# Sliding-window attention with value products that leave queries on partitions, in an order of its own on every engine

## The reference, cut to what matters

```python
qkv = (x @ W_qkv + b_qkv).reshape(B, S, 3, HEADS, HD)      # B=32, S=125, HEADS=8, HD=16
# per head: scores of each query with the keys at most 32 rows away, softmax over them
p = softmax(where(near, q @ k.T * HD ** -0.5, -inf))
attn = p @ v                                               # per head (125, 16)
return attn @ W_proj + b_proj                              # added to h
```

## Time and profile before

| | us |
|---|---|
| median of 3 runs | 592.61 (591.25 to 595.72) |
| profiled execution, its own time | 590.11 |
| its span, first to last instruction or transfer | 588.3 |
| PE / PEld busy | 505.1 / 352.7 |
| DVE / ACT / POOL busy | 417.8 / 371.5 / 272.4 |

### The profile page before, as it was taken

One profiled execution on the slowest core, in us unless ns is written; L12 is line 12 of the kernel. 1 busy time (PEld: TensorE's weight loads), 2 busy tenths in 40 slices (PEclk: granted clock), 3 DMA queues, 4 the chain that ended last, 5 costly groups with the idle time before them and its releaser, 6 DMA issues.

```text
span 588.3 us, 13845 instructions
## 1 busy us (share of the span) xinstructions
PE 505.1 (86%) x4554; PEld 352.7 (60%) x4554; DVE 417.8 (71%) x1694; ACT 371.5 (63%) x1115; POOL 272.4 (46%) x218
## 2 busy tenths in 40 slices
PE   6997999999986999999989999976888888888830
PEld 4686666676654666666666666644666666666510
DVE  3798578888854688878888887635777777777750
ACT  5975588889874344454444445436788888888740
POOL 2760677878865766666665666421111111111030
PEclk9999599999996999999999999986999999999965
DMA  4441122222220000000000000000000000000013
GB/s 153 141 138 37 43 50 59 62 58 59 63 70 29 26 21 31 20 19 20 17 19 20 30 4 1 2 0 0 2 1 3 2 2 2 2 2 2 2 38 103
DMA packets 21914, 19.87 MB, mean 34 GB/s; under 512 B 14180, under 2 KB 18436, under 8 KB 21716
## 3 DMA queue, kind: packets, MB, share of 16 engines
q1 hardware_dynamic: 21268, 18.28, 11.0%
q10 hardware_dynamic: 576, 0.71, 0.4%
HBM read 16.81 MB, written 2.18 MB: 32 GB/s over the span
## 4 chain that ended last, share of the span: by engine, by line
PE 25%; ACT 19%; DVE 9%; POOL 7%; issue 6%; DVEq 0%; ACTq 0%; POOLq 0%
ACT wprobs L977 10%; PE bank L829 6%; DVE n L1112 5%; PE quad L784 4%; POOL hb L1060 3%; POOL hb L1058 3%; PE quad L852 3%; PE bank L909 3%; ACT wprobsT L1003 2%; PE quad L776 2%; ACT oF L995 2%; PE bank L858 2%; ACT woT L1010 2%; ACT ao L942 1%; PE quad L807 1%
## 5 line engine op out<-in xcount | busy, mean ns | idle before, releaser
L476 POOL TENSOR_SCALAR put<-keyb,c 100x1000 f32<-100x1000 bf16 x32 | 89.1, 2784 | 43.6 <-DMA keyb<-key_scratch 27.8
L1078 POOL TENSOR_TENSOR kbd<-wkT,c 128x250 f32<-128x250 f32 x32 | 19.3, 602 | 134.1 <-ACT wkT L985 134.1
L977 ACT ACTIVATE wprobs<-quad,wmax 125x125 f32<-125x125 f32 x256 | 73.1, 384 | 1.8 <-DVE wmax L1166 0.7
L1166 DVE CUSTOM_DVE_ANT_0 quad<-quad,c 125x125 f32<-125x125 f32 x256 | 65.7, 320 | 11.6 <-PE quad L852 8.0
L609 ACT ACTIVATE probs<-quad,negmax 100x250 f32<-100x250 f32 x128 | 58.4, 468 | 19.8 <-DVE negmax L561 18.6
L784 PE MATMUL quad<-h1T,w 128*128 128x500 f32 x128 | 60.7, 598 | 0.4 <-ACT hid L948 0.3
L807 PE MATMUL quad<-w,hid 128*125 128x128 f32 x512 | 59.0, 273 | 0.1
L807 PEld LDWEIGHTS quad<-w,hid 128*125 128x125 f32 x512 | 57.4, 188 | 0.9 <-issue 0.5
L948 ACT ACTIVATE hid<-quad,vec_cols 128x500 f32<-128x500 f32 x64 | 43.0, 676 | 9.8 <-PE quad L784 8.1
L491 PE MATMUL bank<-c,probs 100*125 100x100 f32 x256 | 46.8, 309 | 2.2 <-ACT probs L609 1.4
L491 PEld LDWEIGHTS bank<-c,probs 100*125 100x125 f32 x256 | 35.5, 202 | 19.9 <-issue 12.2
(11 more groups left out here) (138 smaller groups left out, 1227.1 us busy)
## 6 DMA issues: line engine op xcount, KB each, us to landing
keyb<-key_scratch SPq DMA_DIRECT2D x64, 97.7 KB
xa<-xT SPq DMA_DIRECT2D x8, 500.0 KB, 3.6
xt<-xtok SPq DMA_DIRECT2D x16, 250.0 KB
out<-o_all SPq DMA_DIRECT2D x4, 500.0 KB
w<-weights SPq DMA_DIRECT2D x1, 1024.0 KB, 7.3
vec_rows<-rows SPq DMA_DIRECT2D x1, 448.0 KB, 5.4
c<-consts ACTq DMA_DIRECT2D x1, 428.5 KB, 5.9
w<-weights ACTq DMA_DIRECT2D x1, 192.0 KB, 4.4
```

The costliest lines, as they stand in the source:

```text
L476: nc.gpsimd.tensor_scalar(put[u % 3][:, :, :], keyb[p][:, :, :], c[0:ROWS, CONST["sidx"]], None, ALU.is_equal).then_inc(put_done, 1)
L977: ins = nc.scalar.activation(probs[p][:, j, :], s_of(j), ACT.Exp, bias=negmax[p][:, j:j + 1], scale=-1.0)
L1166: ins = nc.vector.tensor_tensor_reduce(s_of(j), s_of(j), c[0:LH, CONST["band"]], 1.0, OFF, ALU.add, ALU.min, negmax[p][:, j:j + 1])
```

## The change

The value product of a head has the transposed probabilities (125 columns) as the stationary operand and the values (now 16 columns and a single column of ones, `VW` = 17) as the moving one. The result has queries on partitions, and the row sum in column 16 of each head. The copy `oT` on ACT and the two transposes L909 go. Reciprocal and normalisation read the products at once, one step later (at the head of DVE's step). The projection writes into the bank of keys, queries and values, with added waits of ACT and PE on `z_done`. `oF` is made by DVE, not ACT. On PE the transpose of `otok` moves behind the transposes of heads 4 to 7, and the projection to between the transposes of heads 0 to 3 and the value products. On ACT the copy of heads 4 to 7 moves between the exponentials of heads 0, 1 and those of heads 2, 3. On DVE z moves behind the minima of heads 4 to 7 and the copy of transposed probabilities ahead of the statistics. The diff, cut to its core:

```diff
 PE
                 if within(u, 2, B + 2):
-                    pe.wait_ge(otok_done, u - 1)
-                    nc.tensor.transpose(y_of, otok[:, :], ident[0:LH, 0:LH]).then_inc(oF_ready, 1)
...
                 if within(u, 2, B + 2):
-                    pe.wait_ge(oF_done, u - 1)
-                    nc.tensor.matmul(y_proj, oF[:, :], w[:, WEIGHT["wp"]], start=True, stop=True).then_inc(proj_ready, 1)
+                    pe.wait_ge(otok_done, u - 1)
+                    nc.tensor.transpose(y_of, otok[:, :], ident[0:LH, 0:LH]).then_inc(oF_ready, 1)
...
+                if within(u, 2, B + 2):
+                    pe.wait_ge(oF_done, u - 1)
+                    pe.wait_ge(v_done, min(u + 1, B))
+                    wait(pe, z_done, u - 2)
+                    nc.tensor.matmul(x_proj, oF[:, :], w[:, WEIGHT["wp"]], start=True, stop=True).then_inc(proj_ready, 1)
+
                 if within(u, 1, B + 1):
-                    wait(pe, z_done, u - 1)
+                    wait(pe, oF_done, u - 1)
                     pe.wait_ge(pT0_done, u)
                     pe.wait_ge(pT1_done, u)
                     pe.wait_ge(v_done, u)
...
                     for j in range(H):
-                        ins = nc.tensor.matmul(y_bank[CW * (j % 4):CW * (j % 4) + CW, LH * (j // 4):LH * (j // 4) + LH],
-                                               vo[pm][:, j, :], probsT[pm][:, j, :], start=True, stop=True)
+                        ins = nc.tensor.matmul(y_o[:, j, :], probsT[pm][:, j, :], vo[pm][:, j, :], start=True, stop=True)
                     ins.then_inc(pv_ready, 1)
-
-                if within(u, 1, B + 1):
-                    pe.wait_ge(oT_done, u)
-                    for i in range(2):
-                        ins = nc.tensor.transpose(y_a[:, 128 * i:128 * i + 128], oT[:, LH * i:LH * i + LH], ident)
-                    ins.then_inc(otok_ready, 1)
 ACT
+                    wait(act, z_done, u - 2)
                     nc.scalar.activation(kT[:, :], x_k, ACT.Identity, bias=col("wk_b")).then_inc(kT_done, 1)
...
-                if within(u, 2, B + 2):
-                    act.wait_ge(oF_ready, u - 1)
-                    wait(act, proj_ready, u - 2)
-                    nc.scalar.activation(oF[:, :], y_of, ACT.Identity, bias=col("wv_b")).then_inc(oF_done, 1)
                 if within(u, 0, B):
                     wait(act, pT0_ready, u - 1)
                     exponents(0)
-                    exponents(1)
                 if within(u, 1, B + 1):
                     act.wait_ge(pT1_ready, u)
                     wait(act, pv_ready, u - 2)
                     nc.scalar.activation(probsT[1 - p][:, 4:8, :]...).then_inc(pT1_done, 1)
                 if within(u, 0, B):
+                    exponents(1)
                     exponents(2)
                     exponents(3)
-                if within(u, 1, B + 1):
-                    act.wait_ge(pv_ready, u)
-                    wait(act, otok_ready, u - 1)
-                    nc.scalar.activation(oT[:, :], y_bank[:, 0:2 * LH], ACT.Copy).then_inc(oT_done, 1)
 DVE, its whole step in the new order
+                if within(u, 2, B + 2):
+                    dve.wait_ge(pv_ready, u - 1)
+                    wait(dve, otok_done, u - 2)
+                    nc.vector.reciprocal(rinv[:, :], y_o[:, :, HD]).then_inc(rinv_done, 1)
+                    dve.wait_ge(rinv_done, u - 1)
+                    wait(dve, oF_ready, u - 2)
+                    nc.vector.tensor_tensor(otok..., y_o[:, :, 0:HD], rinv..., ALU.mult).then_inc(otok_done, 1)
+                if within(u, 0, B):
+                    dve.wait_ge(scores, u + 1)
+                    mask_and_min(0, 4)
+                if within(u, 2, B + 2):
+                    dve.wait_ge(oF_ready, u - 1)
+                    wait(dve, proj_ready, u - 2)
+                    nc.vector.tensor_scalar(oF[:, :], y_of, col("wv_b"), None, ALU.add).then_inc(oF_done, 1)
+                if within(u, 0, B):
+                    mask_and_min(4, 8)
                 if within(u, 2, B + 2):
                     dve.wait_ge(proj_ready, u - 1)
-                    nc.vector.tensor_tensor(z_all..., y_proj.unsqueeze(1), z_all..., ALU.add).then_inc(z_done, 1)
+                    nc.vector.tensor_tensor(z_all..., x_proj.unsqueeze(1), z_all..., ALU.add).then_inc(z_done, 1)
+                if within(u, 0, B):
+                    dve.wait_ge(pT0_ready, u + 1)
+                    wait(dve, pv_ready, u - 1)
+                    nc.vector.tensor_copy(probsT[p][:, 0:4, :]..., t_bank[0]...).then_inc(pT0_done, 1)
                 if within(u, 2, B + 2):
                     dve.wait_ge(z_done, u - 1)
                     nc.vector.bn_stats(zst..., z_all...).then_inc(stat, 1)
```

More of the change, by code:

```diff
@@ L38 @@
 CW = 2 * HD
+VW = HD + 1
 ROWS = 2 * KTOP
@@ L698, in ffn_and_window @@
         kbd = pair("kbd_", [128, 2, LH])
-        vo = pair("vo_", [LH, H, CW])
+        vo = pair("vo_", [LH, H, VW])
         negmax = pair("wmax_", [LH, H])
@@ L702, in ffn_and_window @@
         probsT = pair("wprobsT_", [LH, H, LH])
-        oT = sb("woT", [128, 2 * LH])
         rinv = sb("wrinv", [LH, H])
@@ L719, in ffn_and_window @@
         pT0_ready, pT1_ready, pT0_done, pT1_done = sem("w_pT0_ready"), sem("w_pT1_ready"), sem("w_pT0_done"), sem("w_pT1_done")
-        pv_ready, oT_done, otok_ready, rinv_done, otok_done = sem("w_pv_ready"), sem("w_oT_done"), sem("w_otok_ready"), sem("w_rinv_done"), sem("w_otok_done")
+        pv_ready, rinv_done, otok_done = sem("w_pv_ready"), sem("w_rinv_done"), sem("w_otok_done")
         oF_ready, oF_done, proj_ready, z_done = sem("w_oF_ready"), sem("w_oF_done"), sem("w_proj_ready"), sem("w_z_done")
@@ L727, in ffn_and_window @@
         x_k, x_q, x_v = x_bank[:, 0:LH], x_bank[:, 128:128 + LH], x_bank[0:LH, 256:256 + D]
-        y_a, y_of, y_proj = y_bank[0:LH, 256:512], y_bank[:, 0:LH], y_bank[0:LH, 128:128 + D]
+        x_proj = x_bank[0:LH, 384:384 + D]
+        y_o, y_of = y_bank[0:LH, 0:H * VW].rearrange("p (h f) -> p h f", h=H), y_bank[:, 256:256 + LH]
         def s_of(head):
@@ L1154, in _ @@
             for i in range(2):
-                nc.vector.memset(vo[i][:, :, HD:CW], 1.0).then_inc(ones_in, 1)
+                nc.vector.memset(vo[i][:, :, HD:VW], 1.0).then_inc(ones_in, 1)
             def window(h, p):
@@ L1159, in window, with mask_and_min @@
                 um2, _, _ = shift(h, p, -2)
[L1161 to L1167, removed]
-                if within(u, 0, B):
-                    mask_and_max(0)
-                    mask_and_max(1)
+                def mask_and_min(lo, hi):
+                    for j in range(lo, hi):
+                        ins = nc.vector.tensor_tensor_reduce(s_of(j), s_of(j), c[0:LH, CONST["band"]], 1.0, OFF, ALU.add, ALU.min,
+                                                             negmax[p][:, j:j + 1])
+                        if j % 2:
+                            ins.then_inc(min_done, 1)
+                if within(u, 2, B + 2):
[4 more added lines that the diff above has]
+                    wait(dve, oF_ready, u - 2)
+                    nc.vector.tensor_tensor(otok[:, :].rearrange("p (h f) -> p h f", h=H), y_o[:, :, 0:HD],
+                                            rinv[:, :].unsqueeze(2).to_broadcast([LH, H, HD]), ALU.mult).then_inc(otok_done, 1)
+                if within(u, 0, B):
+                    dve.wait_ge(scores, u + 1)
[6 more added lines that the diff above has]
+                    mask_and_min(4, 8)
                 if within(u, 2, B + 2):
@@ L1175, in window @@
                         dve.wait_ge(h0b_done, NP)
[L1176 to L1182, removed]
+                    nc.vector.tensor_tensor(z_all[:, um2:um2 + 1, :], x_proj.unsqueeze(1), z_all[:, um2:um2 + 1, :], ALU.add).then_inc(z_done, 1)
                 if within(u, 0, B):
@@ L1186, in window @@
                     nc.vector.tensor_copy(probsT[p][:, 0:4, :].rearrange("p h l -> p (h l)"), t_bank[0][0:LH, 0:4 * LH]).then_inc(pT0_done, 1)
[L1187 to L1195, removed]
+                if within(u, 2, B + 2):
+                    dve.wait_ge(z_done, u - 1)
+                    nc.vector.bn_stats(zst[:, um2:um2 + 1, :].rearrange("p a b -> p (a b)"), z_all[:, um2:um2 + 1, :].rearrange("p a b -> p (a b)")).then_inc(stat, 1)
             def spread(lo, hi, count):
```

## The result

The changed kernel takes 647.99 us (643.53 to 655.4), the kernel before beside it 591.93: a ratio of 1.0896, 95% interval 1.0796 to 1.0996. The forecast was slower, by 20 us; it is 56. One of the four executions behind the median (655.4) ran in a slower state; the ratio leaves it out and makes the difference some 53 us (0.0896 x 591.93). The profiled execution is 651.63 us with a span of 649.8, against 590.11 and 588.3.

The account below looks back on a forecast made before the run. No engine is full; a loop of waits across PE, ACT and DVE sets the 4.879 us step. 29 x 0.73 = 21.2, + 0.8 start, - 2.0 end = +20.0 on 592.6: 612.6 us, range 589 to 621.

Parts of the forecast that it names:

- Part 1: PE, transposes of heads 0 to 3 to next scores: 16 load-paced product passes, 0.107 us each; 2.54 us against 2.21.
- Part 2: First minimum to transposes of heads 0 to 3: ACT's copy now stands between exponentials; 2.30 us against 1.88.
- Part 3: Scores to first minimum: reciprocal and normalisation ahead of the minima are covered by the scores' time; stays 0.77 us.
- what I cost at nothing: Window step: oF on DVE, ACT's removed copies, added waits on z and PE's added waits change the step by zero.
- DVE's own loop: DVE, z behind the projection and its queue up to the minima: floor of 4.84 us a step even with free products.
- Start and end: Clip 1's step at low clock adds some 0.8 us; earlier factors and output transfers after clip 31 take off 2.0.
- The sum: Whole kernel: steps, start and end together add 20.0 us to the median 592.6, giving 612.6 us.
- rival 3: PE's clock falls in the window steps: some 3 us a step, up to 700 us, or 620 to 640; chance 0.06.
- Rival 1: Product weight loads hide or go at 25 ns a pass; DVE binds, 589.5 us or 586.5; chance 0.16.
- rival 2: Product loads partly hidden, 0.07 to 0.09 us a pass: step 5.0 to 5.35, time 596 to 605; chance 0.10.

Follow-up runs that it names:

- run 1: Changed kernel with each value product moving 125 columns instead of 17, same weight loads: 614.13 us, ratio 1.0342.
- run 4: Kernel before with only ACT's copy of transposed heads 4 to 7 moved ahead of the exponentials of heads 2, 3: 605.27 us, ratio 1.0204.
- run 7: run 1 with ACT's copy of heads 4 to 7 back behind the exponentials of heads 2, 3: 601.44 us, ratio 1.0143.
- run 6: Changed kernel with seven of eight value products left out, 2 weight loads instead of 16, same 272 columns moved: 584.05 us, ratio 0.9845.
- run 3: Changed kernel plus four extra matmuls of 17 moving columns in PE's pause before the transposes of heads 0 to 3: 660.96 us, ratio 1.1145.
- run 5: Changed kernel with value products moving 64 columns instead of 17: 618.89 us, ratio 1.0434.
- run 2: Changed kernel plus four extra matmuls of 125 moving columns in PE's pause before the transposes of heads 0 to 3: 616.31 us, ratio 1.0383.
- run 10: run 8 with oF on DVE made one pair of minima earlier, before those of heads 6 and 7: 570.92 us, ratio 0.9644.
- run 8: Kernel before, old products, oT's transposes moved behind the next scores; the change's projection bank and oF on DVE; normalisation between minima: 576.89 us, ratio 0.9721.
- run 9: run 7 with the products of heads 0 to 3 moved ahead of the transposes of heads 0 to 3, into PE's pause: 585.58 us, ratio 0.9892.

## Why the prediction was right in part and wrong

1. *Part 1, products by weight loads.* Right: 0.109 us apart at full clock in the changed kernel, forecast 0.107; segment 2.59 for 2.54 (run 1). The matmul L281 was a sound relative. Of the Trainium skill's two rules the load's (TensorE: Matmul & The Clock Gate, LDWEIGHTS, columns over 1.2: an estimated 104 ns) agrees with the trace at full clock to 5%; at the low clock the loads were 0.21 apart. The 60 cycles of the Trainium skill (TensorEngine Tiling, Performance Considerations), an estimated 25 ns, are not what a pass with 125 stationary columns took in any run here.
2. *Part 2, the copy between the exponentials.* Right in kind, 0.05 short: 1.88 became 2.30 in the forecast and 2.35 in runs 1 and 4, and putting the copy back gave 0.475 (run 7). The 0.05 is the 0.64 taken from the earlier trace rows for the start of the exponentials ("With ACT free"); in the steps it stayed at the 0.69 of the earlier trace rows.
3. *Part 3 and what I cost at nothing.* Right where run 1 shows it: scores to minima 0.77. ACT does wait for z there (0.40 us before L982), but its exponentials start by the minima, so neither this nor oF on DVE costs anything.
4. *DVE's own loop.* Forecast 4.84, measured 4.73 (run 6). From z to the first minimum it is 1.43 for 1.58, small instructions being 0.20 to 0.23 apart and not 0.24 to 0.25.
5. *Start and end.* End: at full clock 31.45 us after the last scores in run 1 for 33.69 before, 2.2 less; forecast 2.0. Start: forecast +0.8; run 1 shows +2.4. That the changed kernel shows +0.8 is luck: its step from clip 1 to clip 2 is 1.35 longer (8.47 for 7.12), and its stage happened to begin 0.5 earlier.
6. *The sum.* 612.6 forecast for full clock; run 1, which is the changed kernel with the clock kept, 614.1. Part of this closeness is luck: between the profiled executions the difference is 24.6 us (614.73 less 590.11) where the sum says 20.0, 3.2 more by the steps (5.721 for 5.61) and 1.6 by the start; it was put on a median 2.5 above the profiled execution.
7. *The step that failed* is the one that held the clock at 1.00: rival 3, "The clock falls", was given 0.06 and shut out of the range, on the ground that "its longest pause is about 1.2 us a step" and that all 29 steps before had run at 1.00. Pauses alone were the wrong thing to weigh. Runs 1 and 6 show that a pause of 1.2 to 1.4 us a step does not lower the clock here when the rest of the step moves columns, run 3 that filling it with loads does not raise it (0.72), and runs 1, 5 and 2 that moved columns do raise it, in the products (1.00) or in the pause beside unchanged products (0.98). What lowered it is that the products' 1.7 us of each step went from streamed columns to loads with 17 columns each, on top of the pause that was there; the exact rule is open. The rival's price was about right: "some 3 us a step" at the low clock, measured 8.38 - 5.72 = 2.66 in a step wholly at 0.50. Not foreseen was that the clock alternates, 0.69 in the mean, which gives (6.913 - 5.721) x 29 = 34.6 us, nearly the whole miss of 35.4. Between the profiled executions of the changed kernel and of run 1, 36.9 us apart, the low clock at the end adds 4.0 (35.43 for 31.45), and the earlier start takes back 1.7. The rival named the mechanism ("The new step moves few columns for 1.7 us") and then argued it away with a row that spoke of something else.

Rival 1, cheap loads, did not occur, as L281 had told, and rival 2 did not either.

## What to carry to other kernels

Before an operand swap, count the columns loaded against the columns moved: 16 passes of 125 loaded and 17 moved cost as much as 125 moved, and then ask what the clock does, since such passes leave the array with little to stream. If they can't be avoided, the moving operand can be widened up to the load's length: here that cost nothing (16 loads in 1.83 us either way) and gave 33 to 34 us. A loop of waits cut into segments at three or four starts gave the step of a reordered kernel to within 2.3% in runs 1, 4, 6, 7 and 10, where the clock was kept; for run 8 it gave 4.2 to 4.4 for 4.48. In this loop the gain lay in moving work into an engine's pause (run 9) or a hand-over off the path (run 10), more than in taking instructions away.

## What the runs showed of the hardware that was not expected

- Granted clock over the steps with the same passes and loads: 0.69 with 17 moving columns in the products, 1.00 with 64 and with 125. After the last scores, where the other passes are fewer, it is 0.50 with 64 and 1.00 with 125 (run 5). PE pauses more in the runs that keep the clock: its records are busy 94% of the time with 17 columns (188.63 of 200.49 us) and 82% with 125 (135.99 of 165.91), the low clock itself lengthening the former.
- The clock alternates between its two levels in a steady state, with a pattern that repeats every five steps, for 200 us on end, or, in run 3, once a step.
- Weight loads of 125 columns slow with the clock: 0.109 us apart at 1.00, 0.21 at 0.50.
